# Two value steps in a row, and an earlier start of the constant rows and of the maxima, in a transformer block on one core

## The chip, the cores and the metric

The kernel runs on 1 core of one Trainium2 chip, as one launch. The metric is the device time of an execution in microseconds (us); lower is better. TensorE (PE) multiplies, VectorE (DVE), ScalarE (ACT) and GpSimd (POOL) work on what it leaves in PSUM and SBUF, and SyncE (SP) issues nearly all DMAs. The engines run their own instruction streams in order and meet at semaphores.

## What is computed

The input X is 2 x 1024 x 256 (two batch elements, float32). The reference, cut to what matters:

```python
Xn = layernorm(X) * ln_g + ln_b
Q, K, V = Xn @ Wq + bq, Xn @ Wk + bk, Xn @ Wv + bv        # 16 heads of 16
A = softmax(causal(Q @ K.T / 4))                           # 1024 x 1024 per head
x = layernorm(X + (A @ V) @ Wo + bo)
h = relu(x @ W1 + b1)
alpha = softmax(h @ W2 + b2)                               # 8 experts
out = layernorm(x + sum_k alpha_k * (x @ V_k.T) @ U_k.T)   # rank 64 each
```

## The kernel before

All weights stay in SBUF. A batch element is 8 tiles of 128 rows, in two chunks (c = 0, 1) of 512 rows. The 16 heads are four unit groups (g) of four. What every engine does, and in which order, comes from one list of events, made by `program_order` (L143) and `attention_order` (L58). Each engine's block walks the same list and does its part of each event; so a place in the list is a place in every engine's queue, DMA issues on SP's queue included.

The events around the change:

- `xt`: PE transposes the normalised x (L760), ACT copies it with gain and bias (L526). `qk`: PE projects (L766), ACT writes the bf16 high part (L545), DVE the residue (L640); `part`: ACT the middle part (L550), POOL the low one (L498). Scores are thus computed from bf16 terms stacked in 96 rows. `stack`: SP copies the parts into `stq` and `stk`, 12 issues for one chunk of one group (L448, L449).
- `max`: PE computes scores of a unit and adds the mask (L827, L831), DVE takes the row maxima (L656). A chunk 0 of a group has 11 such units, chunk 1 has 27. `split`: DVE cuts the maxima into bf16 parts (L669 to L672). `rows`: PE transposes them (L837), DVE copies (L679), a DMA (SP L461; for the very first, ACT L535) puts them as three more rows into `stq`. Against them, three rows of `stk` hold -1, written once by ACT at the start (L517), so that a score comes out with its row's maximum taken off.
- `score`: PE (L848) into one of three banks, ACT takes the exp (L559) into one of three `pr` buffers; POOL zeroes the masked triangle of diagonal tiles (L507). A step is one key tile against one chunk of queries for four heads: four `score` events. There are 48 steps per batch element, 8 groups of 4 or 8.
- `value`: PE multiplies probabilities and values of one step (L868), four heads in four 32-column tiles, eight instructions in float32, into a bank of its own. `drain`: ACT copies the bank when a group ends; `turn`: PE transposes it (L878), DVE divides by the sums (L687, L688). A step's exps wait (L557) for the value product three steps back.
- `ot`, `r1`, `ln2`, `x1t`, `h`, `lg`, `weigh`, `alpha`, `vx`, `avt`, `u`, `ln3`: output projection, layer norms and experts. `v` projects the values (L766, copied by ACT L539). The layer norms run on DVE alone.

DVE's events share four PSUM banks in a ring (`DVE_RING`), ACT's share three. PE waits for the bank used four (three) events earlier.

`attention_order` returns an `opening`, the maxima that come before the first score (as many as `course[0]` says), and the rest, in which `target(k)` says how many maxima are to be issued at step k. `beside` puts the other events next to given steps. In `program_order`, the opening of the first batch element follows its projections; that of the second is woven with the expert products of the first (`before`). At the very start ACT waits for the small vectors `cols` (L512), runs one exp so that its table is loaded (L514) and fills the four `stk` (L517).

Of the kernel before, what the change touches and what calls it, by code (L numbers as in the profile page):

```python
# [6 lines left out]
ACT = mybir.ActivationFunctionType  # L7
# [50 lines left out]
def attention_order(b, groups, tiles, beside):  # L58
# [8 lines left out]
    at = [(g, s) for g, c in blocks for s, step in enumerate(steps) if step[0] == c]  # L67
    first_step = [at.index((g, min(s for s, step in enumerate(steps) if step[0] == c))) for g, c in blocks]
    needed = [sum(units[u][0] // TPC == c for u in range(len(units))) for _, c in blocks]
    needed = [sum(needed[:i + 1]) for i in range(len(blocks))]  # L70

    course = [(0, needed[0] + 6), (first_step[1], needed[1] + 12), (first_step[2] - 1, needed[2] + 1), (first_step[-1] - 3, needed[-1])]
    order, issued, due = [], 0, []

    def issue_max(upto):
# [22 lines left out]
    for k in range(len(at) + 3):  # L98
        for j in range(HPG):
# [10 lines left out]
                    order.append((kind, b, at[k - behind][0], steps[at[k - behind][1]][0]))  # L110
            more = beside.get(k, [])
            order += more[j * len(more) // HPG:(j + 1) * len(more) // HPG]
        if 0 < k <= len(at):
            order.append(("value", b, *at[k - 1]))
            g, s = at[k - 1]
    return opening, order


# [18 lines left out]
def woven(*lists):  # L137

    at = sorted(((i + 0.5) / len(l), n, i) for n, l in enumerate(lists) for i in range(len(l)))
    return [lists[n][i] for _, n, i in at]  # L140


def program_order(batches, groups, tiles, parts):  # L143
# [34 lines left out]
    for b in range(batches):  # L178
        nb = b + 1
# [1 line left out]
        mix = [mixture(b, c) for c in range(C)]  # L181
        m = [maps(b, c) for c in range(C)]
        beside = {35: res[0][:parts], 36: res[0][parts:parts + 1], 37: res[0][parts + 1:], 41: mix[0][0], 42: mix[0][1][:parts], 43: mix[0][1][parts:], 44: [("alpha", b, 0)] + m[0][:1], 45: m[0][1:2],
                  46: m[0][2:4], 47: m[0][4:6], 48: m[0][6:7], 49: m[0][7:8], 50: m[0][8:9]}
        if nb < batches:
            beside[30] = [("early", nb)]
            beside[38] = [("ln1", nb, 0, TPC)]
# [9 lines left out]
        qks = begin(b, 1)[parts:]  # L197
        if b == 0:
            at_split = opening.index(("split", 0, 0, 0))
            order += qks + woven(opening[:at_split], vs[0][2:3]) + [opening[at_split]] + vs[0][3:] + opening[at_split + 1:]  # L200
        else:
            order += qks[:3] + woven(qks[3:-1], before[:5], opening[:5]) + qks[-1:]
            order += woven(before[5:], opening[5:], vs[b][:1]) + third[b - 1][1:] + vs[b][1:]
        order += rest
        turned, mixed = mix[1]
        ot, (r4, r6, n) = res[1][:parts], res[1][parts:]
        if nb < batches:
            first, second = begin(nb, 0), begin(nb, 1)
            before = m[1]
            qk, (here, xt, later) = first[parts:-1], (first[-1:], second[:parts], [("stack", nb, 1, 0)])  # L210
            order += qk[:1] + ot + qk[1:2] + m[0][9:10] + [r4, r6, n] + m[0][10:] + qk[2:3] + [("load", nb)]
            order += turned + qk[3:] + here + later + third[b][:1] + xt + mixed + [("alpha", b, 1)]
        else:
            order += ot + [r4, r6, n] + m[0][9:] + turned + mixed
            order += [("alpha", b, 1)] + m[1][:2] + third[b][:1] + m[1][2:-3] + [("ln3", b, TPC, 2)] + m[1][-3:] + [("ln3", b, TPC + 2, 2)]
    return order

# [1 line left out]
def block_kernel(nc, x, vecs, rows, wq, wk, wv, wo, w1, w2, vt, ut, out):  # L219
# [16 lines left out]
    with ExitStack() as ctx:  # L236
# [272 lines left out]

        @block.scalar  # L510
        def _(act):
            act.wait_ge(s_cols, 16)  # L512

            nc.scalar.activation(le[:, 0, 0, 0:1], cols[:, 0, 0:1], ACT.Exp)  # L514
            act.wait_ge(s_one_minus, 1)
            for i in range(STACKS):
                nc.scalar.activation(stk[i][ROWS:ROWS + PARTS].rearrange("p c h s -> p (c h s)").bitcast(F32),  # L517
                                     minus[ROWS:ROWS + PARTS, :].bitcast(F32).to_broadcast([PARTS, C * HPG * CHUNK // 2]),
                                     ACT.Copy).then_inc(s_minus, 1)
            for ev in order:  # L520
                kind, b = ev[:2]
                if kind in ("xt", "ot", "x1t", "h"):
# [438 lines left out]
```

## Time and profile before

| | us |
|---|---|
| median of 3 timed executions | 463.79 (462.13 to 464.18) |
| profiled execution | 466.19 |
| its span in the profile | 464.3 |
| PE busy | 418.5 (90%) |
| DVE busy | 310.2 (67%) |
| ACT busy | 234.3 (50%) |
| POOL busy | 73.3 (16%) |

The profile is of one execution and its rows are read against that execution's time. A busy time is a sum over stages with different bounds; the rows by stage show which engine is full where. A matmul's end is modelled, so that its start, and the start of the next, say more than its duration.

### The profile page before, as it was taken

How to read it: one execution, taken by the hardware profiler on the slowest of the kernel's cores; microseconds unless marked ns; L12 is line 12 of the kernel's file. 1: busy time of each engine (PE TensorE's matmuls, PEld its weight loads, DVE VectorE, ACT ScalarE, POOL GpSimd, SP SyncE). 2: the span in 40 equal slices, each digit the busy share in tenths (PEclk: the TensorE clock that was granted, in tenths of full speed). 3: DMA queues.
4: the chain of work that ended last, by engine and by line, in shares of the span. 5: the costliest groups of instructions: out<-in, count | busy, mean ns of one | idle time of the engine just before them, and what ended most of it. 6: DMA issues, size and time to landing. Idle time of an engine off the chain costs nothing.

```text
span 464.3 us, 7228 instructions
## 1 busy us (share of the span) xinstructions
PE 418.5 (90%) x2541; PEld 209.1 (45%) x2541; DVE 310.2 (67%) x805; ACT 234.3 (50%) x498; POOL 73.3 (16%) x108
## 2 busy tenths in 40 slices
PE   7898896998999989998899987998999989997892
PEld 3355342343344433466457733434334434356452
DVE  5427995888898694326666898688889661126076
ACT  6562553675667575442441453665776665530210
POOL 2132120143021010101130022024021010100000
PEclk9899898999999999999999999899999999999797
DMA  5056662260402000001763135053220000000011
GB/s 182 0 82 96 171 97 39 32 97 12 70 1 93 2 1 0 1 2 43 129 121 48 47 54 87 0 82 59 36 35 3 1 1 2 0 0 1 0 46 45
DMA packets 18435, 21.13 MB, mean 46 GB/s; under 512 B 4960, under 2 KB 11872, under 8 KB 18400
## 3 DMA queue, kind: packets, MB, share of 16 engines
q1 hardware_dynamic: 18349, 20.66, 23.6%
q8 instruction: 20, 0.33, 0.3%
q14 instruction: 15, 0.12, 0.1%
q10 hardware_dynamic: 51, 0.01, 0.0%
HBM read 5.79 MB, written 2.10 MB: 17 GB/s over the span
## 4 chain that ended last, share of the span: by engine, by line
PE 64%; DVE 19%; ACT 7%; SPq 4%; issue 3%; DMA 3%; POOL 1%; DVEq 0%; ACTq 0%
PE ps L766 23%; PE ps L868 13%; PE ps L848 12%; DVE mx L656 9%; PE ps L827 9%; PE ps L831 2%; ACT pr L559 2%; DMA stq<-mrow 2%; PE ps L760 2%; SPq L448 2%; SPq L449 2%; ACT stk L517 2%; DVE st L609 2%; DVE x L616 1%; PE ps L878 1%
## 5 line engine op out<-in xcount | busy, mean ns | idle before, releaser
L559 ACT ACTIVATE pr<-ps 128x512 f32<-128x512 f32 (+3 forms) x384 | 167.3, 495 | 111.3 <-PE ps L848 109.5
L656 DVE TENSOR_REDUCE mx<-ps 128x1 f32<-128x512 f32 (+3 forms) x304 | 182.1, 653 | 34.3 <-PE ps L831 25.5
L848 PE MATMUL ps<-stq,stk 99*128 99x512 bf16 (+3 forms) x384 | 118.5, 336 | 13.8 <-DMA stq<-mrow 8.7
L827 PE MATMUL ps<-stk,stq 96*128 96x512 bf16 (+3 forms) x384 | 115.4, 332 | 2.8 <-DVE mx L656 1.7
L868 PE MATMUL ps<-pr,va 128*32 128x512 f32 (+3 forms) x768 | 82.3, 501 | 0.0
L507 POOL TENSOR_SCALAR_AFFINE_SELECT pr<-pr 128x512 f32<-128x512 f32 x64 | 40.7, 636 | 261.0 <-ACT pr L559 261.0
L848 PEld LDWEIGHTS ps<-stq,stk 99*128 99x128 bf16 x384 | 35.0, 99 | 101.5 <-ACT pr L559 51.6
L831 PE MATMUL ps<-mask,ident_b 128*128 128x128 bf16 x256 | 50.3, 223 | 0.0
L827 PEld LDWEIGHTS ps<-stk,stq 96*128 96x128 bf16 x384 | 38.0, 99 | 21.1 <-issue 6.9
L766 PE MATMUL ps<-pr,w_qk 128*128 128x512 f32 x64 | 30.7, 625 | 2.3 <-ACT pr L526 2.3
L831 PEld LDWEIGHTS ps<-mask,ident_b 128*128 128x128 bf16 x256 | 25.6, 100 | 13.0 <-issue 3.9
L766 PE MATMUL ps<-v_t,x_t 128*128 128x512 f32 x64 | 30.4, 600 | 0.0
L766 PE MATMUL ps<-u_t,avt 128*128 128x256 f32 x128 | 30.2, 382 | 0.0
L640 DVE SCALAR_TENSOR_TENSOR res<-ps,cols,qk_raw 128x512 f32<-128x512 f32 x16 | 12.0, 750 | 25.8 <-ACT qk_raw L545 21.9
L868 PEld LDWEIGHTS ps<-pr,va 128*32 128x32 f32 x768 | 15.3, 108 | 29.3 <-issue 20.5
L498 POOL TENSOR_TENSOR qk_raw<-res,qk_raw 128x512 bf16<-128x512 f32 x16 | 18.3, 1157 | 62.8 <-ACT qk_raw L550 62.8
L725 DVE TENSOR_TENSOR avx<-ps,alpha 128x512 f32<-128x512 f32 x16 | 11.0, 690 | 21.1 <-PE ps L766 21.0
L766 PEld LDWEIGHTS ps<-u_t,avt 128*128 128x128 f32 x128 | 23.4, 190 | 2.9
L545 ACT ACTIVATE qk_raw<-ps,cols 128x512 bf16<-128x512 f32 x16 | 11.0, 687 | 26.9 <-PE ps L766 26.9
L581 ACT ACTIVATE avt<-ps 128x512 f32<-128x512 f32 x16 | 9.5, 597 | 21.8 <-PE ps L913 21.8
L766 PEld LDWEIGHTS ps<-pr,w_qk 128*128 128x128 f32 x64 | 12.3, 199 | 15.6 <-issue 15.3
L766 PE MATMUL ps<-x_t,w 128*128 128x512 f32 x32 | 17.2, 671 | 1.8 <-ACT x_t L531 0.8
(80 smaller groups left out, 346.7 us busy)
## 6 DMA issues: line engine op xcount, KB each, us to landing
stq<-qk_raw SPq DMA_DIRECT2D x32, 96.0 KB, 2.8
stk<-qk_raw SPq DMA_DIRECT2D x32, 96.0 KB, 2.8
x_in<-in_x SPq DMA_DIRECT2D x8, 256.0 KB, 3.6
stq<-qk_raw SPq DMA_DIRECT2D x32, 64.0 KB, 2.4
stk<-qk_raw SPq DMA_DIRECT2D x32, 64.0 KB, 2.4
out_y<-x SPq DMA_DIRECT2D x3, 512.0 KB, 3.0
stk<-qk_raw SPq DMA_DIRECT2D x32, 32.0 KB, 2.4
stq<-qk_raw SPq DMA_DIRECT2D x32, 32.0 KB, 2.2
```

Of the source, the lines that this page charges most:

```text
L498: pool.tensor_tensor(part(w, c, 2)[:, m], res[:, n_part[ev] % RES], part(w, c, 1)[:, m], ALU.subtract).then_inc(s_low, 1)
L507: pool.affine_select(out=blk, in_=blk, compare_op=ALU.is_ge, fill=0.0, base=0, pattern=[[0, HPG], [1, P]], channel_multiplier=-1).then_inc ...
L545: nc.scalar.activation(part(w, c, 0)[:, m], dve_bank(ev), ACT.Identity, bias=cols[:, 2 + w, m:m + 1]).then_inc(s_high, 1)
L559: nc.scalar.activation(probs(b, g, s)[:, j, q0 - c * CHUNK:], act_bank(ev)[:, q0 - c * CHUNK:], ACT.Exp, scale=DH ** -0.5).then_inc(s_act_ ...
L640: nc.vector.scalar_tensor_tensor(res[:, n_high[ev] % RES], dve_bank(ev), cols[:, 2 + w, m:m + 1], part(w, c, 0)[:, m], ALU.add, ALU.subtra ...
L656: nc.vector.tensor_reduce(dst, src, AX.X, ALU.max).then_inc(s_dve_free, 1)
L725: nc.vector.tensor_tensor(avx[:, t % 2, :].rearrange("p (e r) -> p e r", e=E), dve_bank(ev).rearrange("p (e r) -> p e r", e=E), alpha[:, t ...
L766: last = nc.tensor.matmul(out_, lhs(k), rhs(k), start=(k == 0), stop=(k == n - 1))
L827: last = nc.tensor.matmul(bank[:, i * w:(i + 1) * w], q[0:ROWS, t // TPC, j, tile(t % TPC)], k[0:ROWS, k0 // CHUNK, j, 0:w], start=True, s ...
L831: last = nc.tensor.matmul(bank[:, (i + 1) * w - P:(i + 1) * w], ident_b[:], mask[:], start=False, stop=True)
L848: nc.tensor.matmul(bank[:, q0 - c * CHUNK:], stk[stack_of(b, g)][0:ROWS + PARTS, kt // TPC, j, tile(kt % TPC)], stq[stack_of(b, g)][0:ROWS ...
L868: last = nc.tensor.matmul(values_bank[j * VW:(j + 1) * VW, q0 - c * CHUNK:], va[:, kt, g * HPG + j, :], probs(b, g, s)[:, j, q0 - c * CHUNK:],
```

## The change

Value products are issued in even steps only, for the two steps before, one behind the other (before: in each step, for the one before). ACT waits for the constant `minus` alone, does its first exp on it and fills the `stk`, and waits for `cols` after that. In the first batch element the first maxima are woven with three of the four second chunk's projections and no longer follow them; v 4 and v 6 are woven with what comes after the first split. In the second batch element the opening holds 14 maxima beyond the 11 of the first unit group, where it was 6; the four v are woven with the opening, before ln3. The event u 1 moves from step 50 to behind the second projection or, in the second element, behind ln2.

```diff
-    course = [(0, needed[0] + 6), (first_step[1], needed[1] + 12), ...
+    course = [(0, needed[0] + (14 if b else 6)), (first_step[1], needed[1] + 12), ...
...
-        if 0 < k <= len(at):
-            order.append(("value", b, *at[k - 1]))
-            g, s = at[k - 1]
+        if k % 2 == 0 and 0 < k <= len(at):
+            order += [("value", b, *at[k - 2]), ("value", b, *at[k - 1])]
...
-                  46: m[0][2:4], 47: m[0][4:6], 48: m[0][6:7], 49: m[0][7:8], 50: m[0][8:9]}
+                  46: m[0][2:4], 47: m[0][4:6], 48: m[0][6:7], 49: m[0][7:8]}
...
-            order += qks + woven(opening[:at_split], vs[0][2:3]) + [opening[at_split]] + vs[0][3:] + opening[at_split + 1:]
+            order += qks[:2] + woven(qks[2:4], opening[:at_split]) + qks[4:] + [opening[at_split]]
+            order += woven(vs[0][2:], opening[at_split + 1:])
         else:
             order += qks[:3] + woven(qks[3:-1], before[:5], opening[:5]) + qks[-1:]
-            order += woven(before[5:], opening[5:], vs[b][:1]) + third[b - 1][1:] + vs[b][1:]
+            order += woven(before[5:], opening[5:], vs[b]) + third[b - 1][1:]
...
-            order += qk[:1] + ot + qk[1:2] + m[0][9:10] + [r4, r6, n] + m[0][10:] + qk[2:3] + [("load", nb)]
+            order += qk[:1] + ot + qk[1:2] + m[0][8:10] + [r4, r6, n] + m[0][10:] + qk[2:3] + [("load", nb)]
...
-            order += ot + [r4, r6, n] + m[0][9:] + turned + mixed
+            order += ot + [r4, r6, n] + m[0][8:] + turned + mixed
...
-            act.wait_ge(s_cols, 16)
-
-            nc.scalar.activation(le[:, 0, 0, 0:1], cols[:, 0, 0:1], ACT.Exp)
             act.wait_ge(s_one_minus, 1)
+
+            nc.scalar.activation(le[:, 0, 0, 0:1], minus[:, 0:1], ACT.Exp)
             for i in range(STACKS):
                 ...
+            act.wait_ge(s_cols, 16)
```

## Rows read from the trace of the kernel before

**Rows 1.** The page: busy times; the chain by line; two groups, busy us and mean ns.

```profile
PE 418.5 (90%) x2541; PEld 209.1 (45%) x2541; DVE 310.2 (67%) x805; ACT 234.3 (50%) x498; POOL 73.3 (16%) x108
...
PE ps L766 23%; PE ps L868 13%; PE ps L848 12%; DVE mx L656 9%; PE ps L827 9%; PE ps L831 2%; ACT pr L559 2%; DMA stq<-mrow 2%; PE ps L760 2%; SPq L448 2%; SPq L449 2%; ACT stk L517 2%; DVE st L609 2%; DVE x L616 1%; PE ps L878 1%
...
L559 ACT ACTIVATE pr<-ps 128x512 f32<-128x512 f32 (+3 forms) x384 | 167.3, 495 | 111.3 <-PE ps L848 109.5
L656 DVE TENSOR_REDUCE mx<-ps 128x1 f32<-128x512 f32 (+3 forms) x304 | 182.1, 653 | 34.3 <-PE ps L831 25.5
```

**Rows 2.** Busy us by stage: start:end, length, engines, granted clock, DMA share, GB/s.

```profile
110.00:158.00 48.00, 46.56 (x338) 19.89 (x338) 39.75 (x81) 33.47 (x73) 7.86 (x13) 1.00 0.18 40
158.00:196.00 38.00, 35.25 (x204) 15.10 (x197) 21.59 (x86) 21.83 (x52) 4.36 (x7) 1.00 0.01 1
...
236.00:258.90 22.90, 22.90 (x127) 16.22 (x126) 14.60 (x31) 4.20 (x7) 2.29 (x3) 1.00 0.38 68
258.90:270.50 11.60, 10.22 (x60) 6.37 (x59) 10.98 (x39) 5.64 (x13) 1.27 (x2) 1.00 0.14 47
270.50:288.30 17.80, 16.23 (x135) 7.12 (x132) 17.34 (x37) 8.85 (x25) 4.63 (x8) 1.00 0.57 86
```

**Rows 3.** Timeline, the first 15 us: start us, busy us, engine, line, operation.

```profile
0.80 1.28 ACT L514 ACT_TABLE_LOAD   x1 [0.80 <-PEq L951]
0.80 0.10 POOL L470 MEMSET minus<- 128x2 bf16 x1 [0.29 <-POOLq L951]
...
5.62 7.29 ACT L517 ACTIVATE stk<-minus 3x2048 f32<-3x2048 f32 x4
...
11.02 1.24 PE L773 MATMUL ps<-ident_b 128*128 128x512 bf16 x5
...
12.94 1.45 ACT L526 ACTIVATE pr<-ps,cols 128x512 f32<-128x512 f32 x2
...
14.53 8.80 PE L766 MATMUL ps<-pr,w_qk 128*128 128x512 f32 x16 [2.27 <-ACT pr L526]
```

**Rows 4.** Busy us by stretch, where the granted clock (third number from the end) fell.

```profile
14.20:17.60 3.40, 3.07 (x4) 1.30 (x5) 1.30 (x4) 0.19 (x1) 0.00 (x0) 0.61 0.00 0
...
427.30:433.90 6.60, 4.99 (x12) 3.08 (x13) 1.35 (x5) 1.19 (x2) 0.00 (x0) 0.55 0.00 0
```

**Rows 5.** Timeline, from the first split to SP's rows of (0,0,1).

```profile
44.07 0.18 DVE L672 TENSOR_TENSOR mhl<-mres,mhl 128x16 bf16<-128x16 f32 x1
...
48.05 0.38 PE L848 MATMUL ps<-stq,stk 99*128 99x512 bf16 x1 [1.17 <-issue]
...
55.44 0.89 SPq L461 DMA_DIRECT2D stq<-mrow  x1
...
73.67 14.09 SPq L461 DMA_DIRECT2D stq<-mrow  x2
```

**Rows 6.** Timeline of PE around one value group.

```profile
102.76 0.22 PE L831 MATMUL ps<-mask,ident_b 128*128 128x128 bf16 x1
102.91 1.07 PE L868 MATMUL ps<-pr,va 128*32 128x512 f32 x8
103.91 0.28 PE L848 MATMUL ps<-stq,stk 99*128 99x256 bf16 x1
```

**Rows 7.** Timeline, second opening: PE's three v and SP's rows of (1,0,1).

```profile
258.08 5.40 PE L766 MATMUL ps<-w_v,pr 128*128 128x256 f32 x24
...
288.37 0.79 SPq L461 DMA_DIRECT2D stq<-mrow  x1
```

**Rows 8.** Timeline behind the last value group, PE and DVE.

```profile
414.26 1.89 PE L766 MATMUL ps<-u_t,avt 128*128 128x256 f32 x8
...
414.75 0.42 DVE L688 TENSOR_TENSOR x<-ps,rs 128x256 f32<-128x256 f32 x1
...
417.85 3.69 PE L766 MATMUL ps<-w_o,o_t 128*128 128x256 f32 x16 [0.83 <-ACT o_t L531]
...
428.13 1.94 PE L760 MATMUL ps<-ident,x 128*128 128x128 f32 x8 [2.69 <-DVE x L616]
```

More of the change, by code:

```diff
@@ L70, in attention_order @@
     needed = [sum(needed[:i + 1]) for i in range(len(blocks))]
-    course = [(0, needed[0] + 6), (first_step[1], needed[1] + 12), (first_step[2] - 1, needed[2] + 1), (first_step[-1] - 3, needed[-1])]
+    course = [(0, needed[0] + (14 if b else 6)), (first_step[1], needed[1] + 12), (first_step[2] - 1, needed[2] + 1), (first_step[-1] - 3, needed[-1])]
     order, issued, due = [], 0, []
```

## The prediction, as it was made before the change ran

> **What bounds the kernel now.** I read the page's busy times first, then its chain, then the stages, then the timeline where stages meet. TensorE is busy 90% of the span and holds most of the chain; the value products (L868) alone are 13% of the span on it [rows 1]. By stage the picture splits. From 110 to 158 us, with maxima and scores in every step, PE is busy 46.6 of 48 us, but VectorE also 39.8 and ScalarE 33.5: PE is the bound, the others are close. From 158 to 196 us, without maxima, PE is the bound alone. Between the batches PE is full (22.9 of 22.9 us) up to 258.9, then VectorE (11.0 of 11.6, 17.3 of 17.8) until 288.3 [rows 2]. In the first batch's opening PE stands still for ScalarE, and later SP's queue and VectorE are what ends last [rows 3, 5]. So a gain on PE counts in full in some stages and not at all in others.
>
> **Constant rows first on ScalarE.** Before, ScalarE waits for `cols`, fills four `stk` with -1 from 5.62 us on (7.29 us, L517), and only then turns to xt (12.94 us). PE has transposed x by then, has run its warming products to 12.26 us (11.02 + 1.24) and starts the first projection at 14.53. `minus` is written at 0.8 us, by the first POOL instruction, and the table load ends at 2.08 [rows 3]. After, exp and the fills run from 2.1 to 9.6 us, before PE has transposed anything. xt's two copies (1.45 us) can start when their banks are written: the second is, when the products of 11.02 begin, so they end at about 12.2. The projection starts at 12.3 instead of 14.5: **-2.2 us**. PE's gap 12.26 to 14.53 is gone too. Right behind that gap the granted clock falls: from 14.2 to 17.6 us it is 0.61 in the mean (1.2 GHz nearly throughout), with 3.07 us of PE work [rows 4]. At 2.4 GHz that is half: up to **-1.5 us** more. The first stack then starts on SP 3.7 us earlier.
>
> **First maxima among chunk 1's projections.** Eleven maxima of unit group (0,0) used to come after the last projection and around v 4; the split ends at 44.07 + 0.18 = 44.25 [rows 5]. Now they are woven between projections 2, 3 and 4. VectorE has 11 maxima of about 0.6 us (0.653 in the mean of all, [rows 1]; most of these are cheaper) and four residues to do and was idle between residues. From the shifted projections I get a split at about 39.1 to 39.6, **-4.7 to -5.1 us**, of which 3.7 are the first edit. The stack's second half must have landed for unit 0; SP's shifted issues put it there in time. But v 4 and v 6 now stand behind `rows` and between group 1's maxima: 1.8 us each on PE (5.40 us for three, [rows 7]) during which VectorE gets no new bank. The first score, 48.05 before, came 3.8 us after the split's end; now that would be 43.2, and with the two v in PE's queue it is about 44.6 to 45.2. VectorE loses about 2 us of idle time there, but the wait of PE for that DMA (and the half clock behind it) is covered. For the rows of (0,1,0), which release SP's 24 stack issues (between the two L461 at 55.44 and 73.67 us) and so the DMA at 73.67 [rows 5], I take **-3.5 us**, bounds -1.5 (PE idle before the split, 35.4 to 39.1, and half clock under v 4) and -5.1. The split's 24 issues and VectorE's maxima both end with that DMA, both start with those rows, so both shift.
>
> **Value products of two steps in a row.** A group of L868 is eight instructions in 32-column tiles. Row by row: the mask product starts at 102.76 and takes 0.055 us of columns (128 at 2.4 GHz), the group starts at 102.91 and the next score at 103.91 [rows 6]. 0.095 us pass going in; of the 1.00 us inside 0.853 are columns (4 x 512 at 2.4 GHz), so 0.147 go at the end. A pair pays once: **0.24 us per pair** on PE, bound 0 (the second group waits like the first) to 0.24; no two groups stand back to back in this trace. There are 96 groups, 48 pairs, never across a unit group: 11.5 us at most. The Trainium skill (TensorEngine Tiling (Array Packing), Key Properties) says that changing the tiling mode, not just the tile, drains the engine; by it the whole 11.5 us are saved on PE, which the 0.24 us here fit.
> What of it reaches the end: I added up, step pair by step pair, PE's columns, VectorE's maxima and ScalarE's exps at the rows' durations. In steps 8 to 35 the longest engine is PE in some 6 of 14 pairs, VectorE in 6, ScalarE in 2. There a batch gains 1.2 us if the longest sets each pair, 3.3 if PE does throughout. Steps 36 to 47 are PE's: four of six pairs, -1.0; steps 38 to 40 have nothing but scores, and with eight exps (0.50 us each, [rows 1]) in a row on three banks then 2 us of values I charge +0.4. The first eight steps lie under VectorE: nothing. Per batch -2.0, **together -4.0 us**, bounds 0 and -9. Buffers: an exp of step n waits for value n-3; with pairs that value has always been issued before the score, so no wait is added there. POOL's causal selects get more time. Drain and turn keep their places, since every group ends on an odd step.
>
> **More maxima ahead in batch two, v's among them.** Ahead of ln3 PE now also does three v (5.40 us, [rows 7]) and eight more maxima (0.22 to 0.28 us each by their columns, 2.0 us). It is full there [rows 2], so the last u comes 7.4 us later. VectorE has 6.3 us more to do in that time (eight maxima at 0.65, a split and a copy at some 1.1) and 8.3 us of idle time in it (22.9 less 14.6, [rows 2]): it fits. But ln3 starts later by those 7.4 us, and VectorE is then without idle time up to the rows of (1,0,1) at 288.37 [rows 7], as before. 7.4 less 6.3: **+1.1 to +1.3 us**. The scores that PE now does beside ln3 were not late: they still wait for the same rows at 288. PE's queue runs dry beside ln3 for 2 to 3 us; if the clock falls there, VectorE's stage hides most of it. Bounds 0 and +3. SP waits for ln3 ahead of the stack issues, which then end at about 288.8, 0.6 us before VectorE is done: this is the next thing late.
>
> **u 1 behind r1.** At the tail, u (414.26 us, 1.89) stood between turn and ot. VectorE's part of turn is done at 415.17, so ot, o_t and r1 (417.85) come 0.8 us earlier [rows 8] and u moves into ln2's cover: **-0.8 us**. PE's idle time before x1t (2.69 us, to 428.13) shrinks to about 1.1. From 427.3 to 433.9 the granted clock is 0.55 with 4.99 us of PE work [rows 8, 4]. If the shorter gap keeps 2.4 GHz, **-2.5 us** more; even odds and a bit, and I count 1.2 of it. In batch one the move is neutral, PE being full there.
>
> **The sum.** -3.5 - 4.0 + 1.2 - 0.8 - 1.2 = -8.3 us, on the profiled execution (466.19 us, span 464.3). That one is 2.4 us above the median of the three timed; from 463.79 it gives 455.5.
>
> **The rivals.** (a) *Pairs hand their gain on.* VectorE and ScalarE empty the banks no faster, so only PE waits longer for banks; for it speaks that VectorE has 17.3 of 17.8 and 39.8 of 48 us; against it that the chain runs along L868. The time: 463.79 - 3.5 + 1.2 - 0.8 - 1.2 = 459.5. The Trainium skill (the same page, PSUM Bottleneck) says that after a speedup by tiling the copies out of PSUM may become the bottleneck; by that rule it is this case. (b) *Everything counts*: -5.0 - 9 + 0.5 - 3.3 = -16.8, 447. (c) *Slower: bursts starve VectorE.* A pair holds PE for 1.95 us; four full banks carry VectorE for 2.6 us (0.653 each, [rows 1]), but two only for 1.3. If PE enters pairs with two or fewer, VectorE loses 0.65 us in each of some 24 pairs in which it is the longest: +15.6, less the 4.3 of the other edits: 475; with half of them so, 467. It decides from two full banks down. Against it: where VectorE is the longest, PE has filled its ring. (d) *The opening gives nothing* (v 4 and v 6 in front of the first scores, half clock under them) and batch two costs 3: 463.8 - 4 + 3 - 1 = 462.
>
> **Chances.** Forecast 0.46, (a) 0.26, (b) 0.10, (c) 0.07, (d) 0.11. Range 449.5 to 462: (c) and the end of (b) lie outside. About 0.5% is what a measurement can tell from no change here: faster by more (under 461.5) 0.81, within 0.12, slower 0.07.
>
> **What would show it.** After: first projection at 12.3 us with the clock at 1.00 behind it; the split's end near 39.5; first score near 45; the DMA of (0,0,1) near 70; from a pair's start to the next score 1.85 us, not 2.0; in steps 8 to 35 less than 48 us for the same work, by 1 to 3; in batch two the rows of (1,0,1) later, relative to the last attention step of batch one, by about 1 us; r1 0.8 us earlier behind turn, clock at 1.00 under x1t. I am wrong if PE's idle time for banks grows in the dense steps, or if the opening's stage ends at VectorE's wait for PE rather than with SP's issues.

## The result, and the profile after

The changed kernel takes 473.16 us in the median of four (470.7 to 479.84), the one before 463.99 in four; the ratio is 1.018, interval 1.009 to 1.027. Ratios, here and below, leave out executions more than 1.5% above the fastest of their kernel. Forecast were 455.5 us. It is slower, by 4 to 12 us, where a gain of 8 was expected. The profiled execution took 475.5 us, 9.5 us of span more than the one before. Its mean granted clock is 0.958, two others of the four had 0.969 and took 470.7 and 470.8: executions of one and the same kernel differ by how long PE ran at half clock. Before, the profiled execution has a mean of 0.972. If the mean is taken over the span, that is 2 x 0.028 x 464.3 = 26 us at 1.2 GHz before and 2 x 0.042 x 473.8 = 40 us after; work in the 14 us between them would have taken half as long, so at most 7 of the 9.5 us can be clock.

The page of the changed kernel (busy times; the chain by line):

```profile
span 473.8 us, 7229 instructions
...
PE 418.4 (88%) x2541; PEld 214.5 (45%) x2541; DVE 309.7 (65%) x805; ACT 231.2 (49%) x498; POOL 73.3 (15%) x108
...
PE ps L766 25%; DVE mx L656 13%; PE ps L868 13%; PE ps L848 10%; PE ps L827 8%; ACT pr L559 2%; PE ps L831 2%; DMA stq<-mrow 2%; DVE st L609 2%; PE ps L760 1%; DVE x L616 1%; PE ps L878 1%; PE ps L913 1%; DVE nv L601 1%; DVE res L640 1%
...
L868 PE MATMUL ps<-pr,va 128*32 128x512 f32 (+3 forms) x768 | 76.1, 517 | 0.0
```

PE has the same busy time (418.4 against 418.5 us) and a smaller share of a longer span. The value products (L868) take 76.1 us of it, where they took 82.3, so other work of PE shows as many us more, part of it because it ran at half clock. VectorE's maxima hold 13% of the chain, where they held 9%, and SP's issues are gone from it [rows 1]. So no engine got more work: engines wait more, or run slower.

Where the 9.5 us are, stage by stage (a stage ends where SP issues the DMA of the rows named, or where ScalarE's last drain starts, the same events in both kernels):

| stage | before, us | after, us | difference |
|---|---|---|---|
| start to the DMA of rows (0,0,1) | 73.7 | 74.2 | +0.6 |
| to the DMA of rows (0,1,1) | 34.4 | 35.3 | +0.9 |
| to the last rows of batch one, (0,3,1): dense maxima | 51.3 | 51.9 | +0.6 |
| to the last drain: late steps | 40.1 | 41.6 | +1.5 |
| to rows (1,0,1): between the batches and second opening | 88.9 | 96.2 | +7.3 |
| to (1,1,1) | 33.5 | 35.1 | +1.6 |
| to (1,3,1): dense maxima | 51.2 | 51.8 | +0.6 |
| late steps | 40.1 | 39.9 | -0.2 |
| tail | 51.2 | 47.8 | -3.4 |

The changed kernel by these stages (start:end, length, busy us of PE, PEld, DVE, ACT, POOL, granted clock, DMA share, GB/s; from 272.8, where ln3 starts, to the rows of (1,0,1) is the end of the stage between the batches):

```profile
74.20:109.60 35.40, 31.95 (x234) 14.59 (x235) 26.39 (x55) 20.17 (x46) 7.23 (x11) 0.90 0.30 46
161.50:203.00 41.50, 38.41 (x215) 17.05 (x214) 21.50 (x86) 21.09 (x51) 4.46 (x7) 0.96 0.01 1
...
272.80:299.20 26.40, 20.27 (x145) 8.70 (x144) 23.29 (x61) 12.23 (x33) 5.54 (x9) 0.87 0.49 81
299.20:334.30 35.10, 31.21 (x230) 13.86 (x231) 26.05 (x54) 20.23 (x46) 6.72 (x11) 0.90 0.30 47
```

The stage of dense maxima in batch one has the full clock in both kernels, so it shows the order alone. Before, then after, each followed by the value products' part of it (the first two busy times are PE and PEld):

```profile
108.08:159.37 51.29, 49.02 (x356) 20.91 (x355) 42.30 (x86) 34.38 (x77) 9.10 (x14) 1.00 0.17 37
108.08:159.37 51.29, 15.55 (x144) 2.86 (x144) 0.00 (x0) 0.00 (x0) 1.00 0.17 37
109.57:161.46 51.89, 48.72 (x363) 22.06 (x363) 42.34 (x86) 34.34 (x79) 9.09 (x14) 1.00 0.17 37
109.57:161.46 51.89, 13.69 (x144) 3.76 (x144) 0.00 (x0) 0.00 (x0) 1.00 0.17 37
```

The value products take 1.9 us less, and the stage takes 0.6 us more. PE is idle for 3.2 us in place of 2.3, and VectorE for 9.6 in place of 9.0. The first of the prediction's signs of being wrong, that PE's idle time grows in the dense steps, has come.

What answers to [rows 3], the start of the changed kernel:

```profile
2.31 7.30 ACT L516 ACTIVATE stk<-minus 3x2048 f32<-3x2048 f32 x4
10.97 1.45 ACT L526 ACTIVATE pr<-ps,cols 128x512 f32<-128x512 f32 x2 [1.37 <-PE ps L760]
...
12.56 7.10 PE L766 MATMUL ps<-pr,w_qk 128*128 128x512 f32 x16 [0.18 <-ACT pr L526]
```

The projection starts 2.0 us earlier, and its 16 instructions take 7.10 us and not 8.80: no half clock. This part went as forecast. What answers to [rows 5]:

```profile
40.16 0.18 DVE L672 TENSOR_TENSOR mhl<-mres,mhl 128x16 bf16<-128x16 f32 x1
40.39 0.24 PE L837 MATMUL ps<-ident_b,mhl 128*48 128x128 bf16 x1 [3.34 <-DVE mhl L672]
41.04 3.15 PE L766 MATMUL ps<-w_v,pr 128*128 128x256 f32 x8
44.86 1.75 DVE L656 TENSOR_REDUCE mx<-ps 128x2 f32<-128x512 f32 x3 [2.94 <-PE ps L831]
47.58 3.88 DVE L656 TENSOR_REDUCE mx<-ps 128x1 f32<-128x384 f32 x7 [0.97 <-PE ps L831]
...
55.35 3.21 PE L868 MATMUL ps<-pr,va 128*32 128x512 f32 x16
59.05 1.29 DVE L656 TENSOR_REDUCE mx<-ps 128x1 f32<-128x512 f32 x2 [1.91 <-PE ps L827]
...
74.24 0.79 SPq L461 DMA_DIRECT2D stq<-mrow  x1
```

The split ends at 40.3, 3.9 us earlier than before. All of it is gone by 74.2. PE stood 3.34 us in front of the split; v 4 behind it runs at half clock (3.15 us, where v takes 1.8), VectorE waits 2.94 us for it and 0.97 for v 6; then the first pair of value products, at half clock again, takes 3.21 us and VectorE runs out of banks for 1.91. So the second sign came as well: SP's last stack issue ends at 71.4 and the DMA at 74.24 waits for VectorE's copy of 73.95, where before the copy was made at 72.60 and the DMA stood behind SP's issues until 73.67. What answers to [rows 6], and the stretches at half clock:

```profile
92.52 0.22 PE L831 MATMUL ps<-mask,ident_b 128*128 128x128 bf16 x1
92.67 1.92 PE L868 MATMUL ps<-pr,va 128*32 128x512 f32 x16
94.53 0.34 PE L848 MATMUL ps<-stq,stk 99*128 99x384 bf16 x1
```

```profile
41.50:44.90 3.40, 3.40 (x13) 2.44 (x12) 0.47 (x2) 0.60 (x1) 0.00 (x0) 0.52 0.75 109
55.20:58.50 3.30, 3.30 (x17) 0.60 (x17) 1.94 (x4) 0.41 (x2) 0.64 (x1) 0.51 0.28 48
75.60:82.40 6.80, 5.77 (x30) 2.38 (x31) 1.73 (x4) 2.81 (x6) 0.00 (x0) 0.51 0.01 2
184.90:188.30 3.40, 3.40 (x8) 0.88 (x10) 2.99 (x15) 0.96 (x2) 0.63 (x1) 0.51 0.00 0
232.70:236.00 3.30, 3.30 (x6) 1.49 (x6) 1.12 (x6) 0.23 (x1) 0.00 (x0) 0.51 0.73 107
277.10:283.80 6.70, 3.99 (x21) 1.18 (x21) 5.50 (x14) 1.04 (x3) 0.63 (x1) 0.50 0.53 112
301.00:307.70 6.70, 6.17 (x31) 2.54 (x32) 2.12 (x4) 3.21 (x6) 0.00 (x0) 0.50 0.00 0
```

A pair takes 1.86 us start to start, as computed; the saving on PE is real. These seven stretches are 34 us at 1.2 GHz, with 29 us of PE work; an eighth, at the very end, stands in both kernels. The second opening, against [rows 7]:

```profile
272.81 1.38 DVE L609 BATCH_NORM_STATS2 st<-x 128x6 f32<-128x256 f32 x4
279.81 0.61 PE L827 MATMUL ps<-stk,stq 96*128 96x512 bf16 x1 [4.20 <-DVE mx L656]
281.41 2.95 PE L868 MATMUL ps<-pr,va 128*32 128x512 f32 x16
284.90 9.12 DVE L656 TENSOR_REDUCE mx<-ps 128x2 f32<-128x512 f32 x16 [2.16 <-PE ps L831]
...
299.24 0.80 SPq L461 DMA_DIRECT2D stq<-mrow  x1
```

ln3 starts at 272.8 and PE, its scores done, stands still for 4.20 us. The clock falls, the pair behind it takes 2.95 us, VectorE waits 2.16 for its next maximum.

### The profile page after: what moved, and what is told of

Its sections match the earlier page's. It is cut to its first block, busy times and chain, and to the rows that moved or that the text cites. A ratio compares the mean times of both kernels' runs of the same rounds, so it can differ in the third digit from the quotient of the medians.

```text
span 473.8 us, 7229 instructions
## 1 busy us (share of the span) xinstructions
PE 418.4 (88%) x2541; PEld 214.5 (45%) x2541; DVE 309.7 (65%) x805; ACT 231.2 (49%) x498; POOL 73.3 (15%) x108
## 4 chain that ended last, share of the span: by engine, by line
PE 62%; DVE 24%; ACT 6%; issue 4%; DMA 3%; POOL 0%; SPq 0%; DVEq 0%; ACTq 0%
PE ps L766 25%; DVE mx L656 13%; PE ps L868 13%; PE ps L848 10%; PE ps L827 8%; ACT pr L559 2%; PE ps L831 2%; DMA stq<-mrow 2%; DVE st L609 2%; PE ps L760 1%; DVE x L616 1%; PE ps L878 1%; PE ps L913 1%; DVE nv L601 1%; DVE res L640 1%
## 5 line engine op out<-in xcount | busy, mean ns | idle before, releaser
L559 ACT ACTIVATE pr<-ps 128x512 f32<-128x512 f32 (+3 forms) x384 | 164.8, 502 | 121.8 <-PE ps L848 121.3
L656 DVE TENSOR_REDUCE mx<-ps 128x1 f32<-128x512 f32 (+3 forms) x304 | 181.8, 654 | 44.5 <-PE ps L831 29.2
L848 PE MATMUL ps<-stq,stk 99*128 99x512 bf16 (+3 forms) x384 | 119.6, 339 | 15.5 <-DMA stq<-mrow 8.9
L868 PE MATMUL ps<-pr,va 128*32 128x512 f32 (+3 forms) x768 | 76.1, 517 | 0.0
L848 PEld LDWEIGHTS ps<-stq,stk 99*128 99x128 bf16 x384 | 36.0, 99 | 84.9 <-ACT pr L559 30.8
L868 PEld LDWEIGHTS ps<-pr,va 128*32 128x32 f32 x768 | 20.8, 113 | 42.0 <-issue 30.5
L766 PE MATMUL ps<-v_t,x_t 128*128 128x512 f32 x64 | 31.7, 622 | 0.0
L766 PE MATMUL ps<-w_v,pr 128*128 128x256 f32 x64 | 16.6, 406 | 0.3 <-ACT pr L526 0.3
```

The lines of the kernel that those rows point to most:

```text
L559: nc.scalar.activation(probs(b, g, s)[:, j, q0 - c * CHUNK:], act_bank(ev)[:, q0 - c * CHUNK:], ACT.Exp, scale=DH ** -0.5).then_inc(s_act_ ...
L656: nc.vector.tensor_reduce(dst, src, AX.X, ALU.max).then_inc(s_dve_free, 1)
L766: last = nc.tensor.matmul(out_, lhs(k), rhs(k), start=(k == 0), stop=(k == n - 1))
L848: nc.tensor.matmul(bank[:, q0 - c * CHUNK:], stk[stack_of(b, g)][0:ROWS + PARTS, kt // TPC, j, tile(kt % TPC)], stq[stack_of(b, g)][0:ROWS ...
L868: last = nc.tensor.matmul(values_bank[j * VW:(j + 1) * VW, q0 - c * CHUNK:], va[:, kt, g * HPG + j, :], probs(b, g, s)[:, j, q0 - c * CHUNK:],
```

## The experiments

Each is a median beside runs of the kernel before on the same chip at the same time (465.3, 465.9, 464.9, 465.6 and 464.6 us in the five groups of runs). "Of before" is the ratio. Differences in us are between medians unless a ratio is named. Line numbers are up to two higher than before where an edit added lines, and L657 or L850 is then what L656 or L848 is above.

**One part at a time.** Pairs alone:

```diff
-        if 0 < k <= len(at):
-            order.append(("value", b, *at[k - 1]))
...
+        if k % 2 == 0 and 0 < k <= len(at):
+            order += [("value", b, *at[k - 2]), ("value", b, *at[k - 1])]
```

> The kernel before with the value products in pairs and nothing else. Theory: the pair does save 0.24 us of PE (1.86 us for two full groups in the changed kernel), but hands it on in the steps with maxima, and where a pair falls into a stretch at 1.2 GHz it takes about 3.2 us and VectorE runs out of banks (1.9 and 2.2 us in the two openings). So 464 to 469 us, and the steps from the rows of (0,0,1) to the last drain of batch one take the 126 us that they take before, within 1. Rival: the pairs are a gain and the other edits lost it: 458 to 461. Other rival: the pairs carry the whole loss: over 470.

Measured: 472.2 us (five runs, 468.4 to 473.7), 1.014 of before (1.009 to 1.019). The pairs lose on their own, about 6.5 us by the ratio, at the rival's end and not at mine. The profiled execution was the fastest of the five; in it the steps from the rows of (0,0,1) to the last drain took 126.3 us, against 126.9, if one starts at VectorE's copy, and 126.0 against 125.8 from the DMA. So this profile doesn't show where the 6.5 us are.

All but the pairs, that is the whole diff of the change without those lines:

> The changed kernel with the value products back to one in each step. Theory: the loss comes from the openings and from where u was moved, and pairs add 3 to 5 us to it: 464 to 468 us. If the pairs carry the whole loss, this is 455 to 459 (the tail's 3.4 us and the opening's 3.9 us kept). If they save what was forecast, it is 475.

Measured: 473.2 us, 1.015 (1.012 to 1.018), far outside what I expected. The rest loses 7 us without pairs: a loss on both sides, and putting the pairs back on top showed no further difference (473.2 for the whole change). With five runs each I can't say how they overlap.

ScalarE's start alone:

```diff
-            act.wait_ge(s_cols, 16)
-            nc.scalar.activation(le[:, 0, 0, 0:1], cols[:, 0, 0:1], ACT.Exp)
             act.wait_ge(s_one_minus, 1)
+            nc.scalar.activation(le[:, 0, 0, 0:1], minus[:, 0:1], ACT.Exp)
...
+            act.wait_ge(s_cols, 16)
             for ev in order:
```

> The kernel before with only ScalarE's start changed. The first projection starts at 12.3 us and not at 14.5, and the clock stays at 2.4 GHz behind it. Theory: nothing in front of the rows of (0,1,0) takes this back, since the order is that of before, so these rows, SP's 24 stack issues and the rest come 3.5 to 4 us earlier: 460 us. Rival: VectorE or SP takes it back before the first long wait: 463 to 464.

Measured: 463.05 us, 0.995 (0.993 to 0.997): -2.2 us, where I had expected -5. In its profile the rows of (0,1,0) are copied at 50.5 us (55.1 before) and its span is 4.1 us shorter (460.2 against 464.3). That is more than the medians differ: the profile of before carries 3.07 us of PE work at half clock at 14.2 [rows 4], and six of ten profiles with this opening don't (see the end). Those six have these rows at 51.8 to 53.5 us, so that 1.3 to 2.9 us are left for ScalarE's start.

Second opening alone:

```diff
-    course = [(0, needed[0] + 6), ...
+    course = [(0, needed[0] + (14 if b else 6)), ...
...
-            order += woven(before[5:], opening[5:], vs[b][:1]) + third[b - 1][1:] + vs[b][1:]
+            order += woven(before[5:], opening[5:], vs[b]) + third[b - 1][1:]
```

> The kernel before with only the second batch's opening changed (14 maxima ahead, the four v ahead of ln3). Theory: ln3 starts 7.4 us later, VectorE has 6.3 us less to do behind it, and PE stands still beside ln3 so that the clock falls: the rows of (1,0,1) come 1.5 to 4 us later, 465 to 468 us. Rival: the scores done ahead pay it back: 461 to 464.

Measured: 468.5 us, 1.008 (1.005 to 1.011), +3.7 us by the ratio and 3.3 by the medians; in its profile the rows of (1,0,1) are copied 92.1 us behind batch one's last drain (202.5 to 294.6), before 88.6 (199.5 to 288.1). The 3.5 us between them fit the loss. That profile is of the slowest of ten executions; in the stage itself its clock fell once, from 277.8 to 281.3 us, beside ln3, which can be 1.7 of the 3.5.

**The openings taken apart.** ScalarE's start with the first opening as changed:

```diff
-            order += qks + woven(opening[:at_split], vs[0][2:3]) + [opening[at_split]] + vs[0][3:] + opening[at_split + 1:]
+            order += qks[:2] + woven(qks[2:4], opening[:at_split]) + qks[4:] + [opening[at_split]]
+            order += woven(vs[0][2:], opening[at_split + 1:])
```

> ScalarE's start and the first opening as in the changed kernel, all else as before. Beside the run with ScalarE's start alone (463.0 against 465.3 us of before, rows of (0,1,0) at 50.5 us in its profile). Theory: the two v in front of the first score starve VectorE and the wait before the split lets PE's clock fall: rows of (0,1,0) at 54.5 to 56, 466 to 468 us. Rival: the weave is neutral and the loss seen without pairs is from the u moved: 462 to 464.

Measured: 466.9 us, 1.004 (1.000 to 1.008); rows of (0,1,0) at 55.2. The same with v 4 among the maxima and v 6 between split and rows:

```diff
+            order += qks[:2] + woven(qks[2:4], opening[:at_split], vs[0][2:3]) + qks[4:] + [opening[at_split]]
+            order += vs[0][3:] + opening[at_split + 1:]
```

> As the run before, but v 4 stays among the maxima and v 6 between split and rows, as in the kernel before. Theory: with PE's wait for the split covered and no v among group 1's maxima, the rows of (0,1,0) come at 49 to 51 us and the median is 461 to 463.5. Rival: the maxima among the projections cost by themselves (PE waits for the stack's second half): over 465.

Measured: 463.15 us, 0.997 (0.993 to 1.001); rows at 50.9. So the maxima among the projections give nothing over ScalarE's start alone (50.5), and the two v behind the split cost 3.8 us by the medians, 3.0 by the ratios. VectorE in the run with v behind the split:

```profile
41.55 0.69 DVE L657 TENSOR_REDUCE mx<-ps 128x4 f32<-128x512 f32 x1 [0.68 <-PE ps L832]
45.70 1.75 DVE L657 TENSOR_REDUCE mx<-ps 128x2 f32<-128x512 f32 x3 [3.47 <-PE ps L832]
48.35 2.08 DVE L657 TENSOR_REDUCE mx<-ps 128x1 f32<-128x384 f32 x4 [0.89 <-PE ps L832]
```

4.4 us of waiting for PE, and PE had waited 3.34 us for the split; its clock was at half from 38.9 to 45.7. How much of it is order and how much clock, the run with the changed order and dummy products shows (further down): there the clock is full up to 51.7 us and these rows come at 52.8, 2.2 us behind ScalarE's start alone. So about half of the 4.7 us that the rows come later here is the order. The 14 maxima without the moved v, that is the first line of the diff of the second opening alone:

> Only the 14 maxima ahead in the second batch, v as before behind ln3. Both parts of the second opening together cost 3.7 us. Theory: the cost is v ahead of ln3 (5.4 us of PE in front of what VectorE waits for); with v beside ln3 the eight maxima delay ln3 by 2 us and take 6.3 us from behind it, while PE works on v beside ln3, so the clock holds: 461 to 465 us. Rival: the maxima are the cost: 467 to 469.

Measured: 465.2 us, 1.001 (0.998 to 1.003). The maxima are free; of the second opening's 3.3 to 3.7 us some 3 are left for the v ahead of ln3. The u alone:

```diff
-                  46: ..., 50: m[0][8:9]}
+                  46: ..., 49: m[0][7:8]}
...
-            order += qk[:1] + ot + qk[1:2] + m[0][9:10] + ...
+            order += qk[:1] + ot + qk[1:2] + m[0][8:10] + ...
...
-            order += ot + [r4, r6, n] + m[0][9:] + turned + mixed
+            order += ot + [r4, r6, n] + m[0][8:] + turned + mixed
```

> Only u 1 moved. Theory: batch one loses 1.05 us, since u had covered ScalarE's copies of xt for the first projection (0.81 us of waiting in the changed kernel); the tail gains 0.8 us and, if the clock holds under x1t, 2.5 more. 463 to 466 us. Rival: the clock falls in the first gap behind lg, as in the changed kernel at 232.6 us: 467 or more.

Measured: 466.3 us (461.0 to 469.7), 0.999 (0.995 to 1.003), no difference that can be told. In its profile the stage from batch one's last drain to the next split is 2.7 us longer: 1.05 us of u gone as cover, and a fall of the clock from 230.0 to 233.4 us. The fall is not u's doing: it is there from 229.1 and from 226.4 in the runs with late pairs alone and with 14 maxima alone, which leave u in place. The tail behind the last drain took 51.1 us, as before (51.2).

**The pairs taken apart.** In the late steps alone, then in the others alone:

```diff
-        if 0 < k <= len(at):
-            order.append(("value", b, *at[k - 1]))
...
+        if k > 36:                    # the second kernel: if k <= 36
+            if k % 2 == 0 and 0 < k <= len(at):
+                order += [("value", b, *at[k - 2]), ("value", b, *at[k - 1])]
+        elif 0 < k <= len(at):
             order.append(("value", b, *at[k - 1]))
```

> The kernel before with pairs only in steps 37 and later, where there are hardly any maxima. Pairs throughout cost 6.5 us. Theory (VectorE's and ScalarE's banks run dry during a pair where maxima are dense): little here, 463.5 to 466. Rival: the cost is here, since eight exps in a row go through three banks and the clock falls while PE waits for them (batch two lost 1.6 us in these steps): 467 to 469.

Measured: 468.3 us, 1.0045 (1.0015 to 1.007), +2.4 us: the rival's place, not mine.

> The complement: pairs only up to step 36, where maxima are dense. Theory: 468 to 471 us, most of the 6.5 us. Rival: 463 to 466, the cost is in the late steps.

Measured: 465.1 us, 0.999 (0.996 to 1.002), no difference that can be told; I had expected most of the loss here. The profiles are finer. From the DMA of rows (0,1,1) to that of (0,3,1) the stage is at full clock and takes 51.3 us with single products (51.29 before, 51.31 with ScalarE's start alone, 51.30 with late pairs) and 51.9 with pairs (51.87 here, 51.87 with pairs alone, 51.89 in the changed kernel). In batch two it is 51.2 and 51.8. So pairs cost 0.6 us there in each batch. This run's mean clock is 0.979 in the profile, where before had 0.972, which can cover the 1.2 us.

The two halves, -0.8 and +2.4 us, don't add up to the 6.5 us of all pairs. Some 5 us of these stay open; the mean clocks differ (0.961 to 0.971 in the five executions with all pairs, 0.972 to 0.982 in the eleven with dense ones).

Why the late ones lose shows in the timeline of PE in the late-pairs run: h and lg, scores, waits, then

```profile
179.74 0.39 PE L850 MATMUL ps<-stq,stk 99*128 99x512 bf16 x1 [0.26 <-ACT pr L561]
180.34 0.88 PE L850 MATMUL ps<-stq,stk 99*128 99x512 bf16 x2 [0.22 <-ACT pr L561]
181.06 3.40 PE L768 MATMUL ps<-v_t,x_t 128*128 128x512 f32 x4
184.39 2.04 PE L870 MATMUL ps<-pr,va 128*32 128x512 f32 x16
```

The product of v_t takes 3.40 us, otherwise 1.88. Between lg (16 products of 8 columns) and it, the value product that used to stand there is missing. Without the fall the late pairs do gain a little: batch two's late steps, at full clock, take 39.9 us where they took 40.1, batch one's with the fall 41.6. With the product back in place:

```diff
+        if k in (37, 38, 39, 40, 45, 46, 47, 48):   # pairs; steps 41 to 44 as before
```

> Pairs only in the late steps, but with one value product in each of steps 41 to 44, around h and lg. Pairs in all late steps gave 468.3 against 465.9, and in that run's profile the clock fell behind lg (v_t product of 3.40 us instead of 1.88). Theory: the value product between lg and the next scores kept PE busy enough; with it back the loss is gone: 464 to 466 us, no half clock between 160 and 200 us. Rival: the loss is the burst of eight exps on three banks in steps 38 to 40: 467 to 469.

```profile
176.07 1.85 PE L768 MATMUL ps<-w,o_t 128*128 128x8 f32 x16
...
178.30 1.06 PE L870 MATMUL ps<-pr,va 128*32 128x512 f32 x8
...
180.43 0.39 PE L850 MATMUL ps<-stq,stk 99*128 99x512 bf16 x1 [0.32 <-ACT pr L561]
180.66 1.88 PE L768 MATMUL ps<-v_t,x_t 128*128 128x512 f32 x4
```

Measured: 466.7 us, 1.003 (0.999 to 1.006). v_t is back at 1.88 us, and both batches' late steps take 0.6 us less than before in the profile; the median has moved toward before but the interval reaches from a gain to most of the loss. The place is shown in the profiles; that it is the whole of the 2.4 us is not.

The same lateness without adjacency, one product behind the second score and one behind the fourth of even steps:

```diff
+            if j == 1 and k % 2 == 0 and 0 < k <= len(at):
+                order.append(("value", b, *at[k - 2]))
...
-        if 0 < k <= len(at):
+        if k % 2 == 0 and 0 < k <= len(at):
             order.append(("value", b, *at[k - 1]))
```

> Both value products in the even step, as in the change, but the first after the second score and the second after the fourth: as late as in pairs, never side by side. It pays the 0.24 us of a switch each time. If what costs is that PE gives nothing to the other engines for 1.9 us at a stretch, this loses nothing against before: 464 to 467 us. If it is the odd steps without any value product (PE waits for ScalarE, and its clock falls among lg and the scores), this is as slow as the pairs or slower: 469 to 473.

Measured: 484.05 us in the median of four (475.6 to 485.8; the profiled one took 483.8), 2.3% slower even in its fastest, beyond what I expected of any theory. So a loss needs no long burst. That it is the odd steps without any value product that cost is the reading that fits; the run also breaks up every even step once more, and doesn't tell the two apart. In the dense stage of each batch VectorE waits for PE for 12 us in place of 8, and the stage takes 55.5 us in place of 51.3. One fall of the clock is in each, behind PE's wait for the DMA of the rows (1.79 us, 1.28 before), and another behind lg (start:end and clock as above):

```profile
108.50:111.80 3.30, 3.30 (x16) 1.04 (x15) 0.69 (x1) 1.63 (x3) 1.53 (x3) 0.50 0.01 2
183.60:186.90 3.30, 3.30 (x12) 1.01 (x12) 2.89 (x18) 1.90 (x5) 0.00 (x0) 0.50 0.00 0
```

**Clock or order.** The order of before, with dummy products where PE waits; they are extra work, their results are overwritten, nothing of the computation is left out:

```diff
+            def warm(bank, n):
+                for _ in range(n):
+                    nc.tensor.matmul(bank, ident_b[:], ident_b[:].unsqueeze(1).to_broadcast([P, TPC, P]), start=True, stop=True)
...
+                        if g == 0 and c == 1:          # ahead of the wait for the rows
+                            warm(take_act(ev), 10)
...
+                        if c == C - 1 and k == 0:      # ahead of x1t's wait for ln2
+                            warm(bank, 10 if b == NB - 1 else 5)
```

> The order of before, with 10 dummy products (512 columns, into the bank that the next real product overwrites) in front of PE's waits for the rows of (0,1), and 10 (5 in batch one) in front of x1t of the second chunk. Theory: the half clock behind these four waits is gone, each worth up to 1.7 us, the last up to 2.5: 459 to 462 us. Rival: the clock falls elsewhere instead, and PE does the dummies late: 464 to 466.

Measured: 462.4 us (four runs, 459.1 to 464.6), 0.989 (0.979 to 0.999). In its profile:

```profile
75.80:78.90 3.10, 2.04 (x12) 0.86 (x10) 0.35 (x1) 0.51 (x2) 0.00 (x0) 1.00 0.22 33
290.80:294.10 3.30, 3.04 (x24) 1.46 (x25) 1.87 (x4) 2.55 (x6) 0.00 (x0) 1.00 0.00 0
420.00:434.00 14.00, 11.86 (x55) 7.37 (x53) 6.49 (x27) 3.06 (x5) 0.00 (x0) 1.00 0.00 0
...
434.90:438.30 3.40, 3.40 (x8) 1.85 (x8) 1.12 (x6) 0.23 (x1) 0.00 (x0) 0.50 0.00 0
```

The first three stretches had 0.60, 0.60 and 0.78 before. The third fall is not quite gone: 3.4 us at half clock follow at 434.9, where before had 6.8 from 428.0. The same dummies in the changed kernel, and more ahead of its split and beside its ln3:

```diff
+                    if ev == ("rows", 0, 0, 0):
+                        warm(values_bank, 12)
...
+                    if ev == ("score", 1, 0, 2, 0):
+                        warm(values_bank, 14)
```

> The changed kernel with the same dummies, and 12 more in front of its wait for the first split and 14 beside ln3 in the second opening. If the clock carried the loss, it comes to 462 to 466 us. If the order did (v in front of what VectorE waits for, the starved odd steps), it stays at 468 to 472.

Measured: 468.2 us, 1.006 (1.002 to 1.011). Some 5 us of the changed kernel's 473.2 come back, the order of before gains 3 (465.6 to 462.4), and 5.9 us stand between the two even then, where 9.2 stood without dummies. Both theories hold in part: a third of the loss is clock that dummies restore, the rest is order, or falls that the dummies did not reach (the mean clock is 0.979 there and 0.985 in the other, which is 6 us more at half clock, or at most 3 of the 5.9).

**A version that beats both.** ScalarE's start, u 1 behind ln2 in the last batch only, first without and then with the dummies:

```diff
-                  46: ..., 50: m[0][8:9]}
+                  46: ..., 50: m[0][8:9] if nb < batches else []}
-            order += ot + [r4, r6, n] + m[0][9:] + turned + mixed
+            order += ot + [r4, r6, n] + m[0][8:] + turned + mixed
```

> A version meant to beat both: ScalarE's start as changed, u 1 moved behind ln2 in the last batch only, all else as before. The first alone gave 463.05 against 465.3. Theory: r1 comes 0.8 us earlier and the waits behind it shrink; 459 to 462.5 us. Rival: the tail's gain was the clock's luck in one execution: 462.5 to 464.

Measured: 463.1 us (458.0 to 467.9), 0.992 (0.988 to 0.995). That u adds anything to ScalarE's start (0.995, 0.993 to 0.997) is not shown: the intervals overlap, and the tail took 51.1 us in the profile.

> Meant to beat both: ScalarE's start as changed, u 1 behind ln2 in the last batch, the dummies of the run before last, values and openings as in the kernel before. 456 to 459 us if the gains add (2.2, 0.8 to 2, and 3 to 5 for the clock); 461 to 463 if the dummies give nothing.

Measured: 458.2 us (four runs, 457.1 to 459.2), 0.982 (0.975 to 0.989): the fastest. In the profile the clock is 0.989 in the mean. With pairs added to it, throughout and in dense steps only:

> The run with constants, last u and dummies (458.2 us), plus pairs in all steps. Theory: nothing gained where maxima are dense, 1.2 us lost or gained in the late steps as the clock falls behind lg or not: 458 to 462 us. Rival: with the waits filled the pairs save their 0.24 us on PE: 453 to 456. Other rival: pairs cost by starving VectorE at any clock: over 463.

> The same with pairs up to step 36 only. Theory: 457 to 459.5 us, no difference that can be told. Rival (gain on PE): 455 to 457.

Measured: 460.3 us, 0.994 (0.990 to 0.997), and 460.9 us, 0.994 (0.990 to 0.998). These two ran on another chip than the 458.2, so each is held against before on its own: 2 to 3 us more by the medians, up to 5.5 by the ratios, and the intervals just miss each other. So pairs cost something here too, in the dense steps alone as well. The profiled executions have the same mean clock, 0.989 without pairs and 0.990 with all of them, and spans of 456.9 and 457.5 us. From rows (0,0,1) to (0,3,1), first without pairs (458.2 us), then with:

```profile
68.00:152.20 84.20, 81.34 (x595) 35.01 (x594) 68.92 (x142) 55.15 (x124) 16.30 (x25) 1.00 0.24 44
```

```profile
68.60:153.60 85.00, 79.19 (x601) 36.04 (x600) 68.61 (x142) 54.04 (x124) 16.51 (x26) 1.00 0.24 44
```

PE has 2.2 us less to do and the stage is 0.8 us longer. At full clock in both, PE's idle time grew from 2.9 to 5.8 us. That is the forecast's rival (a), and somewhat worse than it: the gain is not only handed on, VectorE gets its banks later too.

## Why the prediction was wrong

**ScalarE's start** was right: 12.56 for 12.3 us, no half clock behind it; alone it is worth 2.2 us in the median, of 3.5 counted for the whole opening.

**First maxima and v** failed, at one step. The split came where computed (40.3, forecast 39.1 to 39.6). But the -3.5 us for the rows of (0,1,0), bounds -1.5 and -5.1, were wrong: they moved by 0.7 us, outside the bounds. I had named the wait before the split, the half clock under v 4 and two v without new banks as the lower bound, and had taken a value between. They all came (3.34, 3.15 and 2.94 us), and the first pair at half clock (3.21 us, 1.91 us of waiting) came on top, which I had put at nothing because "the first eight steps lie under VectorE". The mechanism that I had not carried on to: while VectorE is the bound, PE must keep four banks full, and a pair at 1.2 GHz (3.2 us) takes longer than four banks of maxima last (2.6 us). Also, the -1.5 us for the fall of the clock at 14.2 us counted a fall that six of ten profiles with this opening don't have.

**The pairs.** 0.24 us of PE for each was right (1.86 us from a pair's start to the next score, for 1.85). The 4 us of gain were not there (the terms written down give 1.8 a batch and 3.6 together): +0.6 us a batch in the dense stage at full clock, where -1.2 was forecast for steps 8 to 35; in the late ones -0.2 at full clock, where -1.0 + 0.4 was forecast, and +1.5 with the fall behind lg; 6.5 us of loss for all. The failed step is the sum over step pairs "if the longest sets each pair": it kept each engine's work and let rings and clock be ideal. With the clock held, PE's gain turned up as PE's own waiting (2.9 us idle, then 5.8). The rule of the Trainium skill that was weighed there (TensorEngine Tiling (Array Packing), PSUM Bottleneck: after a speedup by tiling the copies out of PSUM may be the limit) pointed the right way; the trace agrees in that PE's idle time grew while VectorE's work stayed as it was (42.3 us in both dense stages). Rival (c), given 0.07, had the time (467 to 475) by luck: neither its price nor its frequency held. It put 0.65 us on each of 12 to 24 pairs at full clock; nine pairs at full clock cost VectorE 0.6 us together, and two behind falls of the clock cost 1.9 and 2.2 us.

**The second opening.** ln3 came at 272.8, 13.9 us later, of which 6.3 had accumulated before it: 7.6 against 7.4 forecast. "VectorE's stage hides most of it" failed: PE stood 4.2 us beside ln3 (forecast 2 to 3), and the half clock reached the pair behind it. Alone it cost 3.3 to 3.7 us, bounds 0 to 3.

**u 1.** "In batch one the move is neutral, PE being full there" failed: u had covered ScalarE's xt copies and VectorE's turn (PE waits 0.81 us in the changed kernel, `DVE x L688`), and avt came 1.05 us later behind the same start. At the tail the 3.4 us of this execution, for 0.8 and 2.5 forecast, are largely luck: w_o starts 0.6 us sooner behind the last drain (4.1 for 4.7), and no fall of the clock struck before the very end. In three other profiles with u 1 moved (all but the pairs, u alone, ScalarE's start and the last u) the tail took 51.1 us, as before. What answers to [rows 8]:

```profile
430.13 3.69 PE L766 MATMUL ps<-w_o,o_t 128*128 128x256 f32 x16 [0.83 <-ACT o_t L531]
...
440.40 1.06 PE L760 MATMUL ps<-ident,x 128*128 128x128 f32 x8 [0.96 <-DVE x L616]
```

**The range** left out what the experiments found to be a term of the sum: an edit that takes work out of one place leaves a stretch in which PE is less busy, and in some executions the clock falls there (v_t behind lg 3.40 us for 1.88, a pair beside ln3 2.95 for 1.86). I counted the falls that the change would remove (two) and none that it would add.

## What to carry to other kernels

Treat TensorE's clock as a resource that a reordering spends: for each gap that an edit opens on PE, price the work behind it at half clock, and ask who lives from that work. Cheap work in otherwise thin stretches (a value product between lg and the scores, v beside a layer norm, v before a split) does double duty as cover and should not be gathered elsewhere to save a switch of 0.24 us. Where a gap can't be closed, dummy products in it were worth 3 us on the order of before and 5 on the changed one, about as much as the best reordering here. Read the gain or loss of a reordering from stages at full clock, which repeat from run to run to 0.1 us (the dense stage: 51.3 or 51.9), and count the falls of the clock apart.

## What the runs showed that I had not expected

- Two value products in even steps, apart from each other, cost 2.3% in the fastest of four executions and 4% in the median (484 us), side by side 1.4%: the same products, none of them later. The mean clock is 0.949 in the first. By it some 2 x 0.051 x 482 = 49 us ran at half clock, where before 26 did; the 23 us between them can be 12 of the 19 us, the rest is waiting. Why the clock reacts so strongly is not settled.
- One and the same code differs by its execution: up to the first split the run with the second opening alone is the kernel before, and its split came at 46.1 us against 43.4, with 6.8 us at half clock where the other had 3.4 [rows 4]. Ten of the profiles have this opening: in six the clock did not fall there and the split came at 40.9 to 41.7, in two it fell for 3.4 us (43.3 and 43.4), in two for 6.8 (46.1). So the profile that the forecast was worked out from had a fall that six of the ten are without. A single profile is no measure of a change of 3 us; the medians of ten runs were.
